# A Mamba scan stage: keys and values placed ahead of the state's transposes on TensorE and ScalarE

## The reference

```python
x = jnp.einsum('bld,ed->bel', hidden_states, in_proj_w)          # 256 -> 512 channels
x = silu(conv(x, conv_w) + conv_b)                               # u, 4 taps in time
dt_low, Bm, Cm = split(einsum('bdl,ed->bel', x, x_proj_w))       # 16 + 16 + 16 rows
dt = softplus(einsum('brl,dr->bdl', dt_low, dt_proj_w) + dt_proj_b)
def step(state, (d, b, c, u)):                                   # 512 time steps, 16 states
    state = state * exp(d[..., None] * A) + (d * u)[..., None] * b[:, None, :]
    return state, einsum('bdn,bn->bd', state, c)
y = (y + D * u) * silu(z)                                        # z = layernorm(x)
```

## Time and profile before

| what | value |
|---|---|
| median of the runs | 4227.35 us |
| profiled execution, its own time | 4230.01 us |
| its span in the trace | 4228.4 us |
| mean granted TensorE clock | 0.948 of 2.4 GHz |
| TensorE matmul / VectorE / ScalarE busy | 88% / 73% / 40% of the span |
| stage 0 | its scans start from 59.1 to 837.1 us, its last update of x is at 867 us |

### The profile page before, as it was taken

The page is one execution under the profiler, slowest core; times in us unless marked ns, Lnnn a source line. Parts: engine busy times, 40 slices in busy tenths (PEclk is TensorE's granted clock), DMA queues, the critical chain, the costliest instruction groups (busy, mean ns, idle before and its releaser), DMA issues.

```text
span 4228.4 us, 41511 instructions
## 1 busy us (share of the span) xinstructions
PE 3735.9 (88%) x12786; PEld 1938.3 (46%) x12786; DVE 3070.6 (73%) x4986; ACT 1683.3 (40%) x2649; POOL 650.9 (15%) x647
## 2 busy tenths in 40 slices
PE   5989898989999988989974999899999999998656
PEld 3565655644444434434432444455454554553222
DVE  6777777768989784888898754476474673774887
ACT  5767676632322322433330011254353452551322
POOL 1333333433434110333210000000000000000000
PEclk8999999999999999999986999899999999999888
DMA  3323232424242412334422000221021120110000
GB/s 109 116 90 111 90 118 87 179 93 156 83 151 89 150 47 86 109 132 164 165 100 110 1 1 0 71 71 62 27 70 44 45 70 27 62 57 33 10 10 20
DMA packets 89971, 339.96 MB, mean 80 GB/s; under 512 B 11920, under 2 KB 20240, under 8 KB 76080
## 3 DMA queue, kind: packets, MB, share of 16 engines
q1 hardware_dynamic: 59728, 220.61, 14.6%
q0 software_dynamic: 30048, 116.94, 8.1%
HBM read 278.26 MB, written 59.24 MB: 80 GB/s over the span
## 4 chain that ended last, share of the span: by engine, by line
PE 56%; DVE 24%; issue 10%; ACT 6%; DMA 3%; DVEq 0%; POOL 0%; ACTq 0%; SPq 0%; POOLq 0%
PE ps L972 37%; PE ps L1315 5%; PE ps L1046 4%; PE ps L1305 3%; DVE room L1467 2%; PE ps L1192 2%; PE ps L1142 2%; DVE room L1471 2%; PE ps L1039 2%; DVE room L1475 1%; DMA room<-bc_scratch 1%; DVE stat L1429 1%; DVE room L1480 1%; DVE stat L1921 1%; DVE room L1926 1%
## 5 line engine op out<-in xcount | busy, mean ns | idle before, releaser
L972 PE MATMUL ps<-room 128*128 128x512 bf16 (+1 forms) x2912 | 958.5, 487 | 120.4 <-ACT room L920 45.2
L972 PE MATMUL ps<-lnT,room 128*128 128x512 f32 x2240 | 991.2, 598 | 26.3 <-DVE room L1661 11.6
L972 PEld LDWEIGHTS ps<-room 128*128 128x128 bf16 (+1 forms) x2912 | 400.2, 141 | 649.1 <-issue 325.6
L568 POOL TENSOR_TENSOR idle<-idle 128x1 f32<-128x1 f32 x288 | 459.1, 1594 | 1520.5 <-ACT room L773 572.0
L972 PEld LDWEIGHTS ps<-lnT,room 128*128 128x128 f32 x2240 | 427.1, 192 | 574.6 <-issue 533.9
L1142 PE MATMUL ps<-room 128*128 128x512 f32 x864 | 378.4, 595 | 8.5 <-DVE room L1613 8.5
L647 ACT ACTIVATE room<-room,small 128x511 f32<-128x511 f32 x256 | 163.6, 710 | 368.5 <-DVE room L1471 354.6
L972 PE MATMUL ps<-down_rows,room 128*128 128x256 f32 x1024 | 253.0, 403 | 47.0 <-ACT room L767 44.5
L1528 DVE TENSOR_TENSOR_SCAN room<-room 128x2048 f32<-128x2048 f32 x64 | 283.2, 4425 | 6.2
L1471 DVE TENSOR_TENSOR_SCAN room<-room 128x2048 f32<-128x2048 f32 x64 | 283.4, 4428 | 5.4
L1885 DVE TENSOR_REDUCE stat<-ps 128x1 f32<-128x512 f32 x256 | 177.1, 692 | 131.1 <-PE ps L972 131.1
(11 more groups left out here) (217 smaller groups left out, 4917.3 us busy)
## 6 DMA issues: line engine op xcount, KB each, us to landing
kv_stash<-room POOLq DMA_DIRECT2D x128, 256.0 KB, 2.6
room<-in_ffn SPq DMA_DIRECT2D x16, 2048.0 KB, 10.9
room<-bc_scratch POOLq DMA_DIRECT2D x128, 256.0 KB, 3.6
room<-kv_stash SPq DMA_DIRECT2D x64, 512.0 KB, 3.5
room<-stash POOLq DMA_DIRECT2D x24, 1024.0 KB, 9.1
room<-in_ffn SPq DMA_DIRECT2D x20, 1024.0 KB, 4.9
room<-in_ffn SPq DMA_DIRECT2D x12, 1536.0 KB, 8.1
room<-bc_scratch SPq DMA_DIRECT2D x64, 256.0 KB, 3.5
```

The source lines that it names most:

```text
L568: nc.gpsimd.tensor_tensor(idle[:, :], idle[:, :], idle[:, :], ALU.add).then_inc(zeros_added, 1)
L972: last = nc.tensor.matmul(out, lhsT, rhs, start=(i == 0), stop=(i == len(parts) - 1))
```

## The change

On TensorE, keys and values of head n come ahead of the wait for scan n and of the state's transposes, instead of behind them. On ScalarE the tiles of the extras of the state before and the kv tiles are taken ahead of the wait for scan n and the decay; the silu, exp, ln and D times u stay behind the decay and ahead of the taking of h. `take_dt` for the second half moves out of `exp_abs` likewise. The numbers of the tiles follow the new order, and SyncE's wait for the context names the first tile of the new order, which is the same point: all tiles of the batch before are filled.

```diff
@@ mamba_tiles
     for n in range(DS):
-        names += [("h", n, t) for t in range(4)] + [("kv", n, half) for half in range(2)]
+        names += [("kv", n, half) for half in range(2)] + [("h", n, t) for t in range(4)]
@@ SyncE, mamba
                         if n == 0:
-                            sp.wait_ge(tile_filled, tile("h", 0, 0)[0])
+                            sp.wait_ge(tile_filled, tile("kv", 0, 0)[0])
                             sp.dma_start(m_kctx, ctx_d[bass.ds(b * P, P), :]).then_inc(kctx_loaded, 16)
@@ ScalarE, exp_abs
-                    take_dt(m, 1, tile)
                     act.wait_ge(tile_taken, tile("dt", m, NE - 1)[0] + 1)
@@ ScalarE, body
                     for n in range(DS):
+                        if n == 1:
+                            take_inproj(1, front_b, tile)
+                        if n == 3 and not last:
+                            take_inproj(0, front_a, tile)
+                        if n == 4:
+                            take_xd(front_b, 1, b, tile)
+                        if n == 5:
+                            take_dt(1, 0, tile)
+                        if n == 6:
+                            take_dt(1, 1, tile)
+                        if n == 9 and not last:
+                            take_xd(front_a, 0, b + 1, tile)
+                        if n == 10 and not last:
+                            act.wait_ge(sp_corrected, front_b + 1)
+                            take_dt(0, 0, tile)
+                        if n == 11 and not last:
+                            take_dt(0, 1, tile)
+                        if n == 15:
+                            act.wait_ge(stash_stored, b * 48 + 48)
...
+                                nc.scalar.activation(zT3[:, t, :], ps[:, bank, :], ACT.Silu).then_inc(tile_taken, 1)
+                        for half in range(2):
+                            i, bank = tile("kv", n, half)
+                            act.wait_ge(kv_stored[half], b * (H * 16) + n * 16)
+                            act.wait_ge(tile_filled, i + 1)
+                            nc.scalar.activation(m_kv[half], ps[:, bank, :], ACT.Copy).then_inc(tile_taken, 1)
+
                         act.wait_ge(scan_done, b * DS + (n + 1))
                         if n + 2 < DS:
                             decay(n + 2)
...
                         for t in range(NT):
                             i, bank = tile("h", n, t)
                             act.wait_ge(tile_filled, i + 1)
                             nc.scalar.activation(hT3[:, t, :], ps[:, bank, :], ACT.Copy,
                                                  scale=cT3[:, t, DR + DS + n:DR + DS + n + 1]).then_inc(tile_taken, 1)
-                        for half in range(2):
-                            i, bank = tile("kv", n, half)
...
@@ ScalarE, ahead of the batches
                 take_dt(0, 0, first_tiles)
+                take_dt(0, 1, first_tiles)
                 exp_abs(0, first_tiles)
@@ TensorE, body
                     for n in range(DS):
+                        keys_values(b, n, tile)
                         h3 = t3(m_h[n % 2], NE)
                         pe.wait_ge(scan_done, b * DS + (n + 1))
...
                             mm.then_inc(tile_filled, 1)
-                        keys_values(b, n, tile)
                         if n == 0:
                             pe.wait_ge(y_ready, b)
```

More of the change, by code:

```diff
@@ L717, in body @@
                     for n in range(DS):
+                        if n == 1:
[17 more added lines that the diff above has]
+                            act.wait_ge(stash_stored, b * 48 + 48)
+                            for t in range(NT):
+                                i, bank = tile("z", t)
+                                act.wait_ge(tile_filled, i + 1)
[3 more added lines that the diff above has]
+                            act.wait_ge(kv_stored[half], b * (H * 16) + n * 16)
+                            act.wait_ge(tile_filled, i + 1)
+                            nc.scalar.activation(m_kv[half], ps[:, bank, :], ACT.Copy).then_inc(tile_taken, 1)
                         act.wait_ge(scan_done, b * DS + (n + 1))
@@ L724, in body @@
                             decay(n + 2 - DS)
-                        if n == 1:
-                            take_inproj(1, front_b, tile)
                         if n == 3:
                             silu_u(front_b, 1)
[L730 to L735, removed]
                         if n == 6:
@@ L746, in body @@
                         if n == 9:
-                            if not last:
-                                take_xd(front_a, 0, b + 1, tile)
                             ln_w(front_b)
-                        if n == 10 and not last:
-                            act.wait_ge(sp_corrected, front_b + 1)
-                            take_dt(0, 0, tile)
                         if n == 11 and not last:
@@ L756, in body @@
                             ln_w(front_a)
[L757 to L762, removed]
                         for t in range(NT):
@@ L768, in body @@
                                                  scale=cT3[:, t, DR + DS + n:DR + DS + n + 1]).then_inc(tile_taken, 1)
-                        for half in range(2):
-                            i, bank = tile("kv", n, half)
-                            act.wait_ge(kv_stored[half], b * (H * 16) + n * 16)
-                            act.wait_ge(tile_filled, i + 1)
-                            nc.scalar.activation(m_kv[half], ps[:, bank, :], ACT.Copy).then_inc(tile_taken, 1)
                     if not last:
@@ L1087, in mamba @@
                 batches(pe, body)
-                pe.wait_ge(tile_taken, batch_tiles(B - 1, True)("kv", DS - 1, 1)[0] + 1)
+                pe.wait_ge(tile_taken, batch_tiles(B - 1, True)("h", DS - 1, NT - 1)[0] + 1)
             def gate_mamba(stage):
```

## The result

The changed kernel takes 4442.63 us (median of four runs, 4441.9 to 4443.12), against 4227.8 for the kernel before beside it: a ratio of 1.0511, 95% interval 1.0494 to 1.0528. That is 215 us slower, where 227 had been forecast (4454; range 4345 to 4525).

A forecast was written before the change was run, and what follows sets the result against it. TensorE was taken to bound the first stage. The profiled 4230.0 us plus 123 at full clock plus 104 for lost clock made 4457; the profiled execution being 2.7 above the median, 4454 us was forecast, range 4345 to 4525.

The forecast's parts named there:

- The serial chain: First stage: keys and values, their take, decay, side work, h take and identity sums run one after another in each state.
- c: Time from the end of K to the start of S: 3.9 us in a plain state, side work added whole.
- K: TensorE's keys and values of one state, put at 3.45 us at full clock.
- The sum at full clock: Four batches of the first stage, TensorE at full clock: the new order adds 123 us.
- S: TensorE's identity sums of one state, put at 3.43 us from start to start.
- The clock: TensorE loses clock behind gaps in the first stage: 104 us more, bounds nothing and 168.
- The table loads: ScalarE's table loads between K and S: 1.28 us each, the skill page's drain of about 1.38 left out.
- The start of a batch: State 0: K goes into TensorE's 11.35 us wait; S starts about 4.5 us behind the scan, a gain of 3.6.
- Clock unharmed: Rival: TensorE keeps 2.4 GHz through the gaps, 4350 us; chance 0.14.
- Clock mostly low: Rival: TensorE runs largely at 1.2 GHz, some 4880 us throughout, a third of that some 4530; chance 0.08.
- Stores late: Rival: ScalarE's K take waits for GpSimd's store ahead of the decay, +20, 4474 us; chance 0.04.
- Faster, with VectorE late at every state: Rival: TensorE's transposes wait for each scan, which hides K and its takes, 4167 us; chance 0.03.

The follow-up runs named there:

- e1: Changed kernel with ScalarE's wait for scan n and the decay moved ahead of the take of keys and values: 4263.22 us, 1.009 of the kernel before.
- e6: Changed kernel with ScalarE's side work (silu, exp, D times u, ln) moved behind the taking of h: 4347.9 us, 1.0284 of the kernel before.
- e2: Changed kernel with ScalarE's decay, extras' takes and side work ahead of the keys-and-values take, except in state 0: 4161.72 us, 0.9852 of the kernel before.
- e3: Changed kernel with TensorE's waits filled by idle repeats of the last tile's transposes, results unchanged: 4359.29 us, 1.0322 of the kernel before.
- e4: Kernel before, with only state 0's keys and values and their take moved ahead of the waits for scan 0: 4214.16 us, 0.997 of before.
- e5: Kernel before, with only ScalarE's takes of the extras moved ahead of the wait for scan n and the decay: 4360.01 us, 1.0316 of before.

## Why the prediction was right

**The serial chain.** It held in its links and as a whole: c of 3.87 us against 3.9 in a plain state, 7.73 against 7.72 at n = 3, and 85.3 over 15 states in each of the first three batches, against 85.3. Single terms were off by up to 0.15 us, both ways: at n = 4 c is 5.29 for 5.18, at n = 7 6.31 for 6.44. Experiment e1 takes the decay off the chain, e6 the side work, e2 both, and the time falls by 179, 95 and 281 us; e1 and e2 came within 9 us of what had been worked out from the chain, e6 fell by 23 more. What makes the chain is the decay behind K's take, not K ahead of T: e2 keeps TensorE's new order and beats both kernels.

**The sum at full clock**, forecast at +123 us: the result less what the clock took is 215 - 83 = 132 (e3). The third batch lasted 266.1, and less the 22.5 us by which its twelve slow S exceed 3.70 that is 243.5, where 242.0 was forecast. The largest part of the 9 us between them is S itself. It was taken at 3.43 from start to start; behind a wait it lasts 3.54 at full clock (633.24 to 636.78 in the third batch), which makes 6.7 us over 61 states.

**The clock**, forecast at +104 us, was the term that was mis-sized. It is 83 by e3, and 83 again by what the 64 S of the changed kernel take above 3.70. The step that failed took 2.26 us for each of 39 long waits from the one row of before at 4.31 us, 88 in all; they cost 69. In the changed kernel 25 waits of 3.3 to 4.5 us cost a mean of 1.57, three of them nothing, and the 14 above 4.6 cost 2.13. The 19 plain waits cost 0.72 on the mean (8 of them lost the clock), near the 0.85 taken: 14 us for 16. So one term was 9 us too small and the other 21 too large, and it is partly luck that the total came within 11 us of the forecast. S of the changed kernel in a plain state that lost the clock, behind a long wait, and in a plain state that kept it:

```profile
531.58 5.40 PE L1051 MATMUL ps<-room,ident 128*128 128x512 f32 x8 [1.96 <-ACT room L776]
...
547.36 6.47 PE L1051 MATMUL ps<-room,ident 128*128 128x512 f32 x8 [5.18 <-ACT room L776]
...
633.24 3.70 PE L1051 MATMUL ps<-room,ident 128*128 128x512 f32 x8 [1.95 <-ACT room L776]
```

By the rule of the Trainium skill ("TensorE: Matmul & The Clock Gate", on cycling through PSUM's banks), the trace agrees that short idle times between groups make the clock swing. It does not agree that each one does: 11 of 19 short waits cost nothing, and the 131 us worked out by that rule would have been further off than 104.

**The table loads** were taken at 1.28 us. At 647.79 a decay of 2.54 starts, at 650.35 a load of 1.28, and silu begins at 651.64, so no drain stands on the path. The drain that the Trainium skill ("ScalarE: Activation LUTs", on what a table load costs) adds to each switch is not there: by an estimate from that page's 1.38 us, the nine loads of a middle batch would have brought c to 97.7 us over the 15 states, and it was 85.3.

**The start of a batch.** S(0) was put at 4.5 us behind the scan and came at 3.1 to 3.3, at 3.5 in the first batch (3.6 forecast); e4 shows this part by itself as 12 us of gain, which the forecast had at 3.6 us a batch and 0.9 more in the first.

**The rivals.** Clock unharmed fell (0.88 in the stage, and e3). Clock mostly low fell (every recorded K behind state 0 ran at full speed). Stores late fell: no wait of ScalarE for a store is in the list. Faster, with VectorE late at every state, fell: T waited for a scan only at the four batch starts.

**What stays open.** Why some waits lose the clock and others of the same length keep it was not tried. The length alone does not decide: in each of the first three batches a wait of 3.75 us lost 1.70 us at n = 6 and nothing at n = 11. In e2, how much of the stage's rest could still be taken away was not tried either; TensorE is busy there for 699 of the 740 us from 59 to 799.

## What to carry to other kernels

An engine that serves two others in order should do first what needs nothing new. A take that must wait for work not yet done belongs behind the work whose inputs are there, or the engine idles and its next customer pays. Before moving a step ahead of another, write down what ran under what: the decay (2.5 us) was free because it ran under 3.4 us of sums, and the edit moved it to where only 1.75 us of transposes covered it. And a wait that TensorE has in every turn costs more than its length: here 83 us of clock beside the 132 that the order costs at full clock.

## What had not been expected

The price of a lost clock hardly grows with the wait. Waits from 1.9 to 4.5 us cost either nothing or 1.4 to 2.7 us of the S behind them; those of 5.2 cost 2.7 to 2.8, those of 6.6 only 1.6. And moving only the takes of the extras, which the prediction gave no price of their own, cost 133 us by itself (e5).
